# Attention over 4,096 tokens: in every second unit the four output products take all 512 queries at once, between the two products of a maxima tile

## What is computed

```python
def _L0_attn_ref(x, W_down, tokeys, toqueries, tovalues, W_unify, b_unify):
    EMB, HEADS = (256, 16)
    S = EMB // HEADS
    xd = (x @ W_down).reshape(b, t, h, s)
    keys = jnp.einsum('bthk,hik->bthi', xd, tokeys) * scale
    queries = jnp.einsum('bthk,hik->bthi', xd, toqueries) * scale
    values = jnp.einsum('bthk,hik->bthi', xd, tovalues)
    dot = jnp.einsum('bqhs,bkhs->bhqk', queries, keys)
    attn = jax.nn.softmax(dot, axis=-1)
    out = jnp.einsum('bhqk,bkhs->bqhs', attn, values).reshape(b, t, e)
    return out @ W_unify + b_unify
...
x = x + _L0_attn_ref(xn, ...) + _L0_ffn_ref(xn, ...)
x = x + _L1_attn_ref(xn, ...) + _L1_ffn_ref(xn, ...)
```

## Time and profile before

| | us |
|---|---|
| runs before (2) | 3903.76 and 3909.84, median 3906.8 |
| the profiled execution (its span) | 3903.8 |
| of it the loop of units that has maxima tiles | 429.9 to 2916.5 |
| PE busy in the span | 3751.1 (96%), 31,366 matmuls |
| DVE busy | 3315.4 (85%) |
| ACT busy | 2728.3 (70%) |
| POOL busy | 450.1 (12%) |

### The profile page before, as it was taken

How to read it: one execution, slowest core, us unless ns; L and a number is a source line. 1 busy time by engine, 2 the same in 40 slices (tenths; PEclk the granted TensorE clock), 3 DMA queues, 4 the chain that set the end, 5 groups by cost and what they waited for, 6 DMA issues and landing times. The chain is left out here.

```text
span 3903.8 us, 76145 instructions
## 1 busy us (share of the span) xinstructions
PE 3751.1 (96%) x31366; PEld 1950.6 (50%) x31366; DVE 3315.4 (85%) x3513; ACT 2728.3 (70%) x4940; POOL 450.1 (12%) x395
## 2 busy tenths in 40 slices
PE   8799899999999999999999999999999859999998
PEld 6487333333333333333333333333335638888887
DVE  6566799999999999999999999999984847756664
ACT  2454688888888888888888888888886522223332
POOL 0133200000000000000000000000002314102323
PEclk9899899999999999999999999999999979999999
DMA  4810322022122022112202112210013010104332
GB/s 142 235 31 17 111 29 29 6 32 28 11 25 34 10 20 29 20 13 25 32 6 32 28 10 26 33 10 7 10 30 84 1 50 31 32 21 131 78 79 39
DMA packets 301691, 157.87 MB, mean 40 GB/s; under 512 B 218397, under 2 KB 273507, under 8 KB 298800
## 3 DMA queue, kind: packets, MB, share of 16 engines
q1 hardware_dynamic: 289072, 142.49, 19.3%
q0 software_dynamic: 12288, 10.70, 1.7%
HBM read 86.46 MB, written 64.18 MB: 39 GB/s over the span
## 5 line engine op out<-in xcount | busy, mean ns | idle before, releaser
L1208 ACT ACTIVATE probs<-attention_scores_t_sums 128x512 f32<-128x512 f32 x4096 | 2216.6, 597 | 283.0 <-PE attention_scores_t_sums L1132 202.5
L1242 DVE TENSOR_REDUCE max_parts<-attention_scores_q_sums 128x1 f32<-128x1024 f32 x1008 | 1226.0, 1223 | 25.1 <-PE attention_scores_q_sums L1126 20.6
L1242 DVE TENSOR_REDUCE attention_max_parts<-attention_scores_q_sums 128x1 f32<-128x1024 f32 x992 | 1209.3, 1224 | 16.2 <-PE attention_scores_q_sums L1126 11.4
L1132 PE MATMUL attention_scores_t_sums<-q_operand,k_operand 50*128 50x512 f32 x2048 | 753.2, 446 | 14.2 <-ACTq L1222 14.0
L1132 PE MATMUL attention_scores_t_sums<-attention_q_operand,attention_k_operand 50*128 50x512 f32 x2048 | 752.0, 445 | 0.0
L1126 PE MATMUL attention_scores_q_sums<-attention_k_operand,attention_q_operand 48*128 48x512 f32 x2048 | 745.4, 443 | 0.0
L1126 PE MATMUL attention_scores_q_sums<-k_operand,q_operand 48*128 48x512 f32 x1952 | 712.2, 444 | 0.0
L1141 PE MATMUL attention_o_psum_sums<-probs,attention_v_heads 128*32 128x256 f32 x8208 | 655.6, 392 | 3.5 <-ACT o_parts L1204 0.4
L1141 PE MATMUL attention_o_psum_sums<-probs,v_heads 128*32 128x256 f32 x8192 | 654.4, 391 | 3.2
L1126 PEld LDWEIGHTS attention_scores_q_sums<-attention_k_operand,attention_q_operand 48*128 48x128 f32 x2048 | 301.6, 185 | 421.4 <-DVE attention_max_parts L1242 183.1
L1126 PEld LDWEIGHTS attention_scores_q_sums<-k_operand,q_operand 48*128 48x128 f32 x1952 | 288.3, 185 | 403.6 <-DVE attention_max_parts L1242 171.9
(11 more groups left out here) (321 smaller groups left out, 4616.4 us busy)
## 6 DMA issues: line engine op xcount, KB each, us to landing
o_other_half<-o_parts SPq DMA_DIRECT2D x130, 64.0 KB, 2.0
expert_rows<-attention_empty_rows SPq DMA_DIRECT2D x16, 516.0 KB, 5.6
v_scratch<-value_chunk SPq DMA_DIRECT2D x16, 512.0 KB, 5.1
w_whole<-in_L_ffn_ew SPq DMA_DIRECT2D x8, 1024.0 KB, 7.3
experts_w_whole<-in_L_ffn_ew SPq DMA_DIRECT2D x8, 1024.0 KB, 5.4
q_operand<-q_scratch SPq DMA_DIRECT2D x24, 256.0 KB, 4.8
k_operand<-k_scratch SPq DMA_DIRECT2D x24, 256.0 KB, 6.4
attention_q_operand<-q_scratch SPq DMA_DIRECT2D x24, 256.0 KB, 4.8
```

The lines of the kernel that those rows point to most:

```text
L1132: nc.tensor.matmul(ST[bank_n][:, :], KOP[b][64 * h:64 * h + ROWS + 2, kt * P:(kt + 1) * P], QOP[b][64 * h:64 * h + ROWS + 2, c * CH:(c + 1 ...
L1208: nc.scalar.activation(PR[:, tile, :], ST[bank_n][:, :], ACT.Exp).then_inc(st_free, 1)
L1242: nc.vector.tensor_reduce(MPART[par][:, h, u // 4, u % 4:u % 4 + 1], SA[h][:, :], AX.X, ALU.max)\
```

## The change

Line numbers of the changed kernel are two higher than those of before from `pv_half` on. `pv_half`, with a side of 256 queries, becomes `pv_part`, with any slice of the 512 queries. A table `BLOCKS` says after which pair of products a unit's parts of output products stand: in even units as before, queries 0 to 255 after pair (0,1) and 256 to 511 after pair (1,1); in odd units one part with all 512 queries, after pair (1,0). Two units thus have three blocks, not four. The last block of the phase, behind the loop, is one of 512 queries too. `pv_done` is raised once a unit, as before, by the block that ends at query 512. The maxima tiles, their two buffers and the reductions are as they were.

```diff
--- before.py
+++ after.py
@@ -975,6 +975,8 @@
         recip_out = sem("recip_den_out")
         block = ph.block()
         LOAD = 12 * 16
+        LOW, HIGH, ALL = slice(0, CH // 2), slice(CH // 2, CH), slice(0, CH)
+        BLOCKS = ({(0, 1): LOW, (1, 1): HIGH}, {(1, 0): ALL})
 
         def bank(r, u, t):
             return (FIRST + r * ROUND + 4 * u + t) % NB
@@ -1133,15 +1135,15 @@
                                  QOP[b][64 * h:64 * h + ROWS + 2, c * CH:(c + 1) * CH], start=True, stop=True)\
                     .then_inc(st_ready, 1)
 
-            def pv_half(b, u, exps, side):
+            def pv_part(b, u, exps, queries):
+
                 pe.wait_ge(st_free, NB + exps)
-                queries = slice(side * (CH // 2), (side + 1) * (CH // 2))
                 for t in range(4):
                     h, kt = 1 - t // 2, 2 * u + t % 2
                     mm = nc.tensor.matmul(OP[32 * (2 * h + t % 2):32 * (2 * h + t % 2) + 32, queries], VH[b][:, kt, h, :],
-                                          PR[:, u % 4 * 4 + t, queries], start=(u == 0 and side == 0),
-                                          stop=(u == U - 1 and side == 1))
-                if side == 1:
+                                          PR[:, u % 4 * 4 + t, queries], start=(u == 0 and queries.start == 0),
+                                          stop=(u == U - 1 and queries.stop == CH))
+                if queries.stop == CH:
                     mm.then_inc(pv_done, 1)
 
             def unit(i, r, u, last):
@@ -1168,11 +1170,13 @@
 
                             used = n + 1 if (r, u, t) != (0, 0, 0) else n + NB
                             score_tile(1 - half, tb, tc, 2 * t_unit + j, used, bank(r, u, t))
-                    if half == 0 and u == 1:
-                        pe.wait_ge(o_copied, g + 1)
-                        if r % NQ == 0:
-                            pe.wait_ge(v_in[r // NQ % 2], (i + 1) * 16)
-                    pv_half((r - (u == 0)) // NQ % 2, (u - 1) % U, count(i, r, u - 2, 3) + 1, half)
+                        if (half, j) in BLOCKS[u % 2]:
+                            if u == 1:
+                                pe.wait_ge(o_copied, g + 1)
+                                if r % NQ == 0:
+                                    pe.wait_ge(v_in[r // NQ % 2], (i + 1) * 16)
+                            pv_part((r - (u == 0)) // NQ % 2, (u - 1) % U, count(i, r, u - 2, 3) + 1,
+                                    BLOCKS[u % 2][half, j])
 
             pe.sem_inc(loaded[0], LOAD)
             pe.sem_inc(v_in[0], 16)
@@ -1193,8 +1197,7 @@
                         unit(i, r, u, last)
 
             halves(body)
-            for side in range(2):
-                pv_half(1, U - 1, count(NP // 2 - 1, HALF - 1, U - 2, 3) + 1, side)
+            pv_part(1, U - 1, count(NP // 2 - 1, HALF - 1, U - 2, 3) + 1, ALL)
 
         @block.scalar
         def _(act):
```

## The result

The changed kernel takes 4212.62 us (median of 2 runs, 4211.39 to 4213.85) against 3906.8: **a ratio of 1.078 (95% interval 1.076 to 1.080)**. The forecast was 4203 within 4140 to 4255, slower. Its profiled execution has a span of 4212.0 us, 308.2 more than the one of before.

What follows compares the result with a forecast made beforehand. TensorE was taken as the bound before; after, head 1's buffer loop, 5.50 us per two units for 4.92. 3903.8 + 290 + 8 − 4 = 4197.8, plus 3 for the median, 4201, stated as 4203; range 4140 to 4255.

Steps and rivals of the forecast that it cites:

- The bound before: In the loop with maxima tiles, TensorE sets the pace at 1.23 us per half unit; VectorE has 0.10 to spare.
- TensorE's saving: In TensorE's queue, three blocks in place of four: two units take 4.58 us in place of 4.92, worth 170 us.
- The chain: Closed loop over head 1's maxima buffer, the long block between its two products: 5.50 us for two units, before 4.92.
- The sum: Whole kernel: +290 us for 1,000 units with maxima, +8 for seams and start, −4 for the last units: 4197.8.
- The rest of the program: The last 24 units, which have no maxima and no chain: 12 × 0.34, so −4 us.
- a seam: Between the 62.5 rounds: small reduction 0.29 and copy up to 0.23 us, 0.52 added to the chain each round.
- The turn with the small reduction: Unit 7 of a round: reducing the 512 maxima lies in the chain and adds 0.29 us a round.
- the one with the copy: Units 0 and 1: copying `OP` delays the score tile of unit 1's pair (1,0), up to 0.23 us more.
- the two small additions behind the sum: Added to 4197.8: 3 us because the profiled run lies under the median, giving 4201, then rounding up to 4203.
- The clock: Rival: TensorE waits 0.92 of 5.50 us, so its clock falls; 4272 with a tenth of the loop at half clock; 4%.
- That TensorE stays the bound: Rival in TensorE's queue: the 170 us saving comes, giving 3733 us; chance 4%.
- The change is absorbed: Rival: saving and VectorE's 0.4 us slack cover the wait, chain within 0.15 of 4.92, 3830 to 3980 us; 3%.

Runs made afterwards that it cites:

- the first experiment: Changed kernel with odd units' 512-query block split into 256 queries after pair (0,1) and 256 after pair (1,0): 4081.64 us, ratio 1.045.

## Why the prediction was right, step by step

**The bound before** was TensorE: halving the reductions leaves it at 3907.84 us against 3910.49 in the same series.

**TensorE's saving.** The block of 512 at full clock takes 1.00 us (2007.71 to 2008.71), as worked out from two rows at half clock, and two units 4.59 with the short reductions, where the terms gave 4.58.

**The chain.** Each term came out as taken: 0.05, 0.43, 1.00, 0.53 (I took 0.54), 1.13 and 1.13, 1.22, and between them and the next load 0.05 to 0.07. The median of all turns is 5.505 us, predicted 5.50. VectorE's idle time is 0.89 in a turn, as predicted, and 472 us in all, where I said some 450.

**The sum.** Loop +311.8 us against the +298 that I summed up (290 and 8). The rest of the program is 3.6 shorter, where I took 4, and the spans differ by 308.2. A round is 44.59 us by the median; 8 × 5.505 = 44.04 of it, so a seam costs 0.55 and not 0.52. The turn with the small reduction is 0.28 longer than the others, as taken (0.29); the one with the copy is 0.29 longer, where I said up to 0.23: the copy starts 0.12 behind the block's last product by the median, and I had taken 0.05. That and the 0.005 of a turn are some 5 us. The other 9 lie with the clock, below. Of the two small additions behind the sum, the 3 us for the median didn't come (the profiled run is 1.2 over the median this time), and the 2 from 4201 to 4203 had no term behind them.

**The clock.** I held a fall of TensorE's clock for a rival with a price of 69 us if it took a tenth of the loop. It did come, five times in the 2,798 us, each for a few us; in the traces of the kernel before and of the ten others it never did so behind the first 50 us of the loop. Two windows of the changed kernel, 10 us apart; the last three numbers are granted clock, DMA share and GB/s:

```profile
2037.00:2042.00 5.00, 4.43 (x39) 1.29 (x36) 4.62 (x4) 4.24 (x8) 0.00 (x0) 1.00 0.93 105
...
2047.00:2052.00 5.00, 5.00 (x34) 1.45 (x26) 2.68 (x4) 3.03 (x7) 1.28 (x1) 0.67 0.14 31
```

0.67 in the mean of the second means that TensorE had 1.2 GHz in a part of it. VectorE's timeline there:

```profile
2042.54 4.62 DVE L1245 TENSOR_REDUCE max_parts<-attention_scores_q_sums 128x1 f32<-128x1024 f32 x4 [0.88 <-PE attention_scores_q_sums L1128]
2049.48 1.23 DVE L1245 TENSOR_REDUCE max_parts<-attention_scores_q_sums 128x1 f32<-128x1024 f32 x1 [2.32 <-PE attention_scores_q_sums L1128]
```

2049.48 − 2042.54 = 6.94 us for a turn of 5.51. Each of the five costs 1.4, together 7 us. The loop's mean is still printed as 1.00. Ahead of the fall TensorE had worked 4.43 us in 5, with waits of 0.3 to 0.4 us before some of the maxima products. That is its share in the whole loop as well (2501.20 of 2798.45), so these rows don't show what made the clock fall there. In the first round the clock also took longer to rise: that round is 47.7 us, 3.2 over the median, where before the change it was 1.4 over it. The change isn't shown to be the cause of this: in the profiled run of the control with short reductions and the blocks of before, the first round is 51.9 us, 12.1 over its median. So this rival did not decide anything, but the clock is 9 of the 14 us that the sum was short by.

**The other rivals.** That TensorE stays the bound was wrong in the changed kernel and right as a statement of what the change could give: 3777 with short reductions, where I wrote 3733 for it. Of the 44 us between them some 31 are seams that I hadn't priced for that rival: the trace has a turn of 5.45 instead of 4.60 once in a round, in units 0 and 1, so a seam is 0.86 where it was 0.36 before the change. Some 9 are the median turn, 4.60 for 4.58. *The change is absorbed* fell with the length of the chain, 5.505. The Trainium skill's rule that a change of tiling mode drains the engine (TensorEngine Tiling, "Key Properties") fits TensorE's part of it: three blocks in place of four gave 4.59 for 4.92. No run here separates a drain from the weights that aren't loaded in advance. The rule says nothing on the buffer's loop.

## What to carry to other kernels

When a block of work is moved in an engine's queue, list the buffers whose filling or refilling it now lies in, and sum the closed chain *release, refill with all that stands between, handover, drain*; compare it with the pace of the busiest engine, not with the engine's idle time. A chain can be cut by handing the buffer over in smaller pieces, and only the buffer in the chain needs it: here that turned +7.8% into −2.4%, and with the blocks of even and odd units exchanged into −3.6%. What an edit saves on the bound engine may be lost to another engine that has little to spare, here 0.10 us in 1.23, so name that slack in us per step before counting the gain.

## What I had not expected of the hardware

The granted clock of TensorE fell to 1.2 GHz for a few us at five places of a loop in which TensorE was busy 2501.20 us of 2798.45 and its longest wait for a reduction was 0.9 us. In the kernel before and in the ten others it never did so between 500 us and the end of the loop, also not in the first experiment, which has a block inside the filling and where TensorE was busy 1886 us of the 2000 from 700 on. The turns ahead of the five falls look like all others, 5.50 to 5.51 us long in four cases and one with the small reduction in the fifth, so what made the clock fall at these places and not elsewhere isn't shown. Each fall cost 1.4 us.
